# Attention's last four iterations: two scans of the gate move from before to behind the third head's first low parts on VectorE

## The reference

```python
x = x + attn(cond(x, fside, fside, w1, u1, cond_512), Wq, bq, Wk, bk, Wv, bv, Wo, bo)
x = x + ffn(cond2(x, fside, fside, w2, u2, cond_512), gate_w, w_gate, w_up, w_down, sw_gate, sw_up, sw_down)
```

## Time and profile before

| | |
|---|---|
| median of three runs | 2279.98 us (2278.03 to 2283.61) |
| time of the profiled execution | 2272.61 us |
| its span in the trace | 2270.9 us |
| mean granted TensorE clock | 0.977 |
| TensorE busy | 2141.2 us, 94% of the span |
| VectorE busy | 1357.4 us, 60% |
| ScalarE busy | 1160.4 us, 51% |
| GpSimd busy | 1431.8 us, 63% |

### The profile page before, as it was taken

How to read it: one execution, slowest core, us unless ns; L and a number is a source line. 1 busy time by engine, 2 the same in 40 slices (tenths; PEclk the granted TensorE clock), 3 DMA queues, 4 the chain that set the end, 5 groups by cost and what they waited for, 6 DMA issues and landing times. The chain is left out here.

```text
span 2270.9 us, 39956 instructions
## 1 busy us (share of the span) xinstructions
PE 2141.2 (94%) x11247; PEld 1860.2 (82%) x11247; DVE 1357.4 (60%) x2501; ACT 1160.4 (51%) x2491; POOL 1431.8 (63%) x953
## 2 busy tenths in 40 slices
PE   3999999999999999989899989999999999999996
PEld 2788888888878878777777879889999999998875
DVE  8778888888856686666765533333333333333386
ACT  5587777777767777767663123333333333333310
POOL 8787778778755666666672321466586868653365
PEclk9899999999999999989998999999999999999998
DMA  5633445443365546665345553566666676664666
GB/s 135 182 101 122 134 132 169 156 135 102 113 226 167 158 151 192 210 208 168 123 133 199 205 166 108 159 182 191 179 194 201 194 203 189 201 192 128 178 208 203
DMA packets 367657, 380.29 MB, mean 167 GB/s; under 512 B 51556, under 2 KB 283560, under 8 KB 362728
## 3 DMA queue, kind: packets, MB, share of 16 engines
q1 hardware_dynamic: 256520, 252.46, 36.1%
q10 hardware_dynamic: 95584, 75.01, 10.7%
q0 software_dynamic: 15360, 50.34, 6.8%
HBM read 264.21 MB, written 120.59 MB: 169 GB/s over the span
## 5 line engine op out<-in xcount | busy, mean ns | idle before, releaser
L2113 POOL TENSOR_SCALAR we_high<-we_raw 128x1408 fp32r<-128x1408 f32 (+1 forms) x94 | 132.1, 1405 | 304.8 <-PE up_e L708 232.0
L2115 POOL TENSOR_TENSOR we_low<-we_raw,we_high 128x1408 fp32r<-128x1408 f32 (+1 forms) x94 | 312.1, 3321 | 7.8
L2328 DVE TENSOR_TENSOR hidden_e<-silu_e,up_e 128x352 f32<-128x352 f32 x127 | 66.2, 521 | 250.3 <-ACT silu_e L2267 250.3
L2311 DVE TENSOR_TENSOR hT_low<-hT_ps,hT_high 128x256 fp32r<-128x256 f32 x127 | 53.9, 425 | 252.8 <-ACT hT_high L2253 252.8
L2267 ACT ACTIVATE silu_e<-gate_e 128x352 f32<-128x352 f32 x127 | 59.0, 465 | 284.0 <-PE up_e L708 272.1
L708 PE MATMUL gate_e<-we_high,xT_high 128*128 x508 | 176.2, 347 | 11.3 <-DVE xT_low L2318 6.4
L2272 ACT ACTIVATE rows_out<-down_e 128x512 f32<-128x512 f32 x127 | 75.9, 598 | 197.4 <-PE down_e L708 197.2
L708 PE MATMUL gate_e<-we_high,xT_low 128*128 x508 | 164.5, 324 | 0.0
L708 PE MATMUL up_e<-we_high,xT_high 128*128 x508 | 164.1, 323 | 0.0
L708 PE MATMUL gate_e<-we_low,xT_high 128*128 x508 | 164.0, 323 | 0.0
L708 PE MATMUL up_e<-we_high,xT_low 128*128 x508 | 163.6, 322 | 0.0
(11 more groups left out here) (403 smaller groups left out, 7197.4 us busy)
## 6 DMA issues: line engine op xcount, KB each, us to landing
slots_out<-rows_out ACTq DMA_DIRECT2D x127, 256.0 KB, 2.4
rows_early<-slots_in ACTq DMA_DIRECT2D x500, 64.0 KB
we_raw<-L_ffn_w_gate SPq DMA_DIRECT2D x32, 704.0 KB, 4.8
we_raw<-L_ffn_w_up SPq DMA_DIRECT2D x32, 704.0 KB, 5.0
w_ring<-L_attn_Wq SPq DMA_DIRECT2D x64, 256.0 KB, 3.1
q_T<-q_out SPq DMA_DIRECT2D x64, 256.0 KB, 2.5
w_ring<-L_attn_Wk SPq DMA_DIRECT2D x64, 256.0 KB, 3.5
w_ring<-L_attn_Wv SPq DMA_DIRECT2D x64, 256.0 KB, 3.7
```

Of the source, the lines that this page charges most:

```text
L2113: nc.gpsimd.tensor_scalar(wh[:, p, at:to], raw[:, at:to], 1.0, 1.0, ALU.mult, ALU.mult).then_inc(w_hi, 1)
L2115: nc.gpsimd.tensor_tensor(wl[:, p, at:to], raw[:, at:to], wh[:, p, at:to].bitcast(F32), ALU.subtract).then_inc(w_split, 1)
L2328: nc.vector.tensor_tensor(hb[:], sg[:], psu[:], ALU.mult).then_inc(h_done, 1)
```

## The change

In the third list of `DVE_ORDER` the token `ha` moves three places back. Before, VectorE ran the two numerator scans right after the next iteration's first keys (`k0`) and ahead of the last head's reciprocal (`i3`), the third head's first two low parts (`a2`) and the second head's low average (`A1`). Now these three come first, then the two scans, then the third head's last low part (`b2`) and the denominator's scans (`hb`). No instruction is added or removed, and no other engine's list is changed.

```diff
@@ -436,7 +436,7 @@
 DVE_ORDER = (
...
-    "M0 mD0 i0 V0 V1 V2 a0 M1 mD1 mX0 hm V3 b0 mW0 i1 K2 mD2 K3 M2 a1 mA0 A0 mP0 i2 mP1 b1 mP2 mP3 M3 mX1 k0 ha i3 a2 A1 b2 hb mW1 a3 A2 b3 k1 A3 mA1 hd O0 hr O1 hR O2 hf O3".split(),
+    "M0 mD0 i0 V0 V1 V2 a0 M1 mD1 mX0 hm V3 b0 mW0 i1 K2 mD2 K3 M2 a1 mA0 A0 mP0 i2 mP1 b1 mP2 mP3 M3 mX1 k0 i3 a2 A1 ha b2 hb mW1 a3 A2 b3 k1 A3 mA1 hd O0 hr O1 hR O2 hf O3".split(),
 )
```

## The result

The changed kernel takes 2291.11 us (median of 20 runs, 2279.78 to 2298.82), the kernel before 2282.47 us on the same chip (20 runs, 2278.03 to 2288.20): a ratio of 1.0032, 95% interval 1.0021 to 1.0044. It is slower by about a third of a per cent, 7 us by the ratio and 8.6 us by the medians, where 4 us faster was forecast. The time lies above the forecast range, and the sign is wrong.

The account below looks back on a forecast made before the run. TensorE, busy 94% of the span, was taken as the bound, so only its stops or low clock could be won. Terms −5.0 + 0.45 − 0.5 + 0.9 = −4.15 took 2279.98 to 2275.8 us; range 2270.5 to 2283.0.

Parts of the forecast that it names:

- Iteration 12, −5.0 us: TensorE's wait before `b2` goes, `a3` comes 2.9 us earlier, `A3` starts 5.0 us earlier; bounds 2.9 to 6.8 won.
- the wrong place for the clock: In iteration 12, `L1` was taken at the high clock, 1.3 us for 2.55; `A3` was left at the low level.
- second rival: TensorE leaves `b2` earlier but stands in `A2` and before `b3`; clock stays low: −1.0 us, 2279.0 us, chance 0.2.
- Iteration 13, +0.45 us: Nothing in front gets earlier; 0.8 us left on `a3` and `b3`, about half swallowed: 0.45 lost, between 0 and 1.6.
- the idle 1.54 before `a3` absorbs its part: Iteration 13: VectorE's idle time absorbs part of the pair's 2.4 us, leaving 0.8 us on `a3` and `b3`.
- Iterations 14 and 15, −0.5 and +0.9 us: 14: `a3` earlier, 0.5 won, between 1.1 won and 1.7 lost; 15: 0.9 lost, between 0.2 and 2.0.
- The meeting in 14: In iteration 14 the moved pair of scans meets GpSimd's L999; 0.7 us booked.
- The meeting of `hb` in 15: In iteration 15 `hb` slides into GpSimd's `wO_low`, which it missed by running early; 0.7 us booked.
- Does the gain reach the end?: After `A3`, the next iteration's weights have 6.6 us of room for 5.0, so what TensorE wins arrives.
- third rival: Slower: the pair's new place meets GpSimd in each iteration, 2.7 us more than alone: +5.2, 2285.2 us, chance 0.12.
- The base: The runs' median was put 7.4 us above the profiled execution, 2272.61, so the forecast starts from 2279.98 us.

Follow-up runs that it names:

- after_both: Changed kernel with the last three indirect transfers issued an iteration later and `wO_low` behind the gate's sums, against the kernel before: ratio 1.0005, a second time 1.0008.

## Why the prediction was wrong

**Iteration 12, −5.0 us.** The wait before `b2` did go. Three steps failed. First, the term rested on a state that the kernel before is in only part of the time: the pair of 3.00 + 2.22 us stands in six of the eight traces with the old order in iteration 12; in the other two the pair takes 2.4, as in the kernel before run again, and TensorE doesn't wait before `b2` at all:

```profile
971.28 1.22 DVE L1503 TENSOR_TENSOR_SCAN g_nf<-par,g_ekv 128x512 f32<-128x512 f32 x1
972.41 1.20 DVE L1504 TENSOR_TENSOR_SCAN g_nb<-par,g_ekv 128x512 f32<-128x512 f32 x1
...
974.61 0.44 PE L1122 MATMUL weights_T<-ident,prob 128*128 128x128 f32 x2
```

Second, what TensorE won before `b2`, 2.4 us, and what it won behind it went into new waits: 0.80 us in `A2` and 2.3 more before `b3`. TensorE came to `b3` early, but VectorE was the one to be waited for: the first low part of `a3` came 1.6 us earlier relative to the fourth head's scores, not 2.9, since the exponentials and with them the low parts of `a2` were 0.8 us later than I had booked, and `hb` took 3.3 us beside `wO_low` and not 2.4. Third, I had the wrong place for the clock. With the first stop gone the clock did stay at its high level at once: from `b2` to the end of `A2` it was 1.00, where the kernel before had 0.59, and `A2` took 2.2 us of work for 3.7. But `L1` and `A3` stand behind the second stop, and there it was 0.50: `L1` took 2.56 us, as before. `A3` started 2.45 us earlier relative to the fourth head's scores, not 5.0. The low stretch then reached on into the output products, to 998.1, where in the kernel before it ended in the last products of `A3`, and the next iteration's scores came only 1.35 us earlier. That is near the second rival's mechanism, "the stop only moves"; I gave it 0.2 on the ground that 2.65 us are more than all that stands behind can take back. The new waits took back 3.1.

**Iteration 13, +0.45 us.** Measured +3.17, above the upper bound of 1.6. The step that failed is the price of what is left after "the idle 1.54 before `a3` absorbs its part": the first low part of `a3` came 1.5 us later, about the 0.8 of the forecast and the 1.0 us of `hb` beside `wO_low`, which I had looked for in iteration 15 only. And I priced the stop by its length; for the clock behind it the bound had 1.2 us at most. `b3` came 1.5 us later, and from `b3` to the next scores it took another 1.7. In eight us from `b3` on the granted clock was 0.79 before and is 0.50 after, the low level of 1.2 GHz for the whole stretch (before, then after; the columns are us, busy time with counts of the five engines, granted clock, DMA share, GB/s):

```profile
1056.30:1064.30 8.00, 7.45 (x36) 6.55 (x37) 3.45 (x7) 2.89 (x6) 6.56 (x6) 0.79 0.72 174
1064.30:1073.10 8.80, 8.80 (x40) 7.29 (x39) 6.24 (x7) 5.32 (x7) 5.33 (x4) 1.00 0.79 277
```
```profile
1057.80:1065.80 8.00, 7.98 (x30) 7.40 (x31) 2.79 (x5) 2.42 (x5) 5.47 (x5) 0.50 0.94 241
1065.80:1076.30 10.50, 10.50 (x46) 8.61 (x45) 8.10 (x9) 5.06 (x7) 8.58 (x8) 0.96 0.85 297
```

In `after_both`, where the stop before `b3` is 1.93, the same eight us have 0.79 again, and iteration 13 takes 65.2. So here 1.0 us more of stopping, from 1.93 to 2.96, came with the clock's fall, and the two make up nearly all of the 3 us. Over all traces a stop of 2.95 us or more before `b3` was followed by 0.50 to 0.62 each time, twelve times in iterations 12 and 13. But 1.93 us were followed by 0.79 four times and by 0.61 or 0.62 twice, and 1.03 or 1.04 us in the kernel before run again by 1.00, 0.79 or 0.59: the length of the stop alone does not tell the clock.

**Iterations 14 and 15, −0.5 and +0.9 us.** Measured +0.38 and +1.59, both inside their bounds. The meeting in 14 came as booked, 1.87 us for the first scan; its price stands in `A2`, a wait of 1.42. The meeting of `hb` in 15 came too, 2.00 us. The times themselves prove little: in the traces with the old order iteration 15 takes 58.3 to 61.5 us. In the one run with the order in 15 alone the median says 4.0 us.

**Does the gain reach the end?** Here the largest part of the loss was missed. The step that failed: I asked only what the next iteration could lack because TensorE arrives earlier, found room in the weights, and booked nothing for what VectorE meets there. It was TensorE and VectorE that arrived later, by 3 us, while GpSimd did not: its row of four subtractions came 5.0 us after the first scores in place of 7.6, onto the choice that VectorE does there in iteration 14. The held operation costs 4.4 us of waiting for `v_low`, and 6.7 us at a granted clock of 0.58 follow it; in sum it is 6.5 us more from first to second scores than in the trace before. That is a meeting of VectorE with GpSimd, the mechanism of my third rival, but at a place an iteration away from the scans and at five times the 1.2 us that I gave one meeting. (That rival's sum is zero at 1.4 us of meetings in each iteration, not at 1.2: the forecast has two of 0.7 us in it already.)

**The base.** The profiled execution of before lay 10 us under the median of 20 runs, not 7.4. Of the 15.3 us between forecast and result, 2.5 are the base of three runs; the rest is the change, 8.6 lost where 4.15 won was forecast. That execution had the short stretch behind attention, 148 us. On the last chip, where the kernel before takes 2283 us, all traces have 160, and on the three where it takes 2266 to 2268, 147 to 148. So most of the 10 us may be this stretch; no run shows it for the chip of the result.

What stays open: why 15 alone costs 4 us in the median, why 13 and 15 together cost more than the whole change, and how often the old order, too, is caught at the start of iteration 14. Its traces show holds of 0 to 4.62 us there; the two with a start of 17.4 and 17.5 us have an iteration 13 of 62, so that the long start costs little there.

## What to carry to other kernels

A stop that a move takes away is won only so far as nothing stands behind that is just as late: follow the moved work to its new place, and add what the engines that run free of it will then run into, an iteration further on as well. An operation that had a place in another engine's waiting time is free there, and the empty idle time in the new trace (3.22 us here) is the first sign that it was. And take a term of several us from more than one execution: here the largest was there in six traces of eight.

## What was new of the hardware

A VectorE operation with its inputs in SBUF can be held by a whole row of GpSimd operations, not by one. Conversions and two-input operations of 8 to 16 elements per partition, 0.17 to 0.30 us alone, were there for 5.86 to 5.96 us beside four GpSimd subtractions without a gap, for 4.62 beside three (and one of 128x512, 0.74 us alone, for 5.17), and for 1.3 to 2.3 where an indirect transfer or the end of the work followed one or two. In the rows above the held operation began up to 0.65 us before the first of the four. The Trainium skill (SBUF — State Buffer, Who interferes with whom) has a GpSimd operation and a VectorE operation with two SBUF inputs, or one in a two-port mode, exclude each other, the loser waiting for the other to finish. The trace agrees on which operations are touched: conversion and two-input operations are, the reciprocal, with one input, was not (0.18 us). Low parts with one input in PSUM aren't either: in iteration 13 of the kernel before two of them took 1.29 us from 1055.53 on the earlier trace rows, beside this one:

```profile
1055.39 1.29 POOL L984 TENSOR_TENSOR wO_low<-w_ring,wO_high 128x512 fp32r<-128x512 f32 x1
```

On the length the measurement goes further than the page: the wait was for the row and not for its first operation.
